# Ternary-weight gated feed-forward stage: biases accumulated on TensorE, Silu read from PSUM, one product per half, first rounding step on ScalarE

## What is computed

```python
def bit_linear(x, w, b):
    gamma_x = clip(max(abs(x), axis=-1), 1e-05)
    x_dq = clip(round(x * 127 / gamma_x), -128, 127) * gamma_x / 127
    gamma_w = clip(mean(abs(w)), 1e-05)
    w_dq = clip(round(w / gamma_w), -1, 1) * gamma_w
    return einsum('bsd,hd->bsh', x_dq, w_dq) + b
gate = silu(bit_linear(x, gate_w, gate_b))     # 256 -> 1024
val = bit_linear(x, val_w, val_b)              # 256 -> 1024
y = bit_linear(gate * val, out_w, out_b)       # 1024 -> 256, own maximum for each token
x = x + tanh(g_ffn[2]) * y
```

## Time and profile before

| What | us |
|---|---|
| median of 3 runs | 1729.23 |
| lowest, highest run | 1728.65, 1737.1 |
| the profiled execution, its own time | 1737.16 |
| span of the profiled execution | 1735.4 |
| bit stage, from the first `ints(0)` to the last `finish` | 986.9 to 1174.1 |

### The profile page before, as it was taken

One profiled execution on the slowest core, in us unless ns is written; L12 is line 12 of the kernel. 1 busy time (PEld: TensorE's weight loads), 2 busy tenths in 40 slices (PEclk: granted clock), 3 DMA queues, 4 the chain that ended last, 5 costly groups with the idle time before them and its releaser, 6 DMA issues.

```text
span 1735.4 us, 20241 instructions
## 1 busy us (share of the span) xinstructions
PE 1288.0 (74%) x6664; PEld 724.3 (42%) x6670; DVE 1071.7 (62%) x2575; ACT 455.5 (26%) x632; POOL 307.6 (18%) x287
## 2 busy tenths in 40 slices
PE   0011899999979989967767445554888889899997
PEld 0000545454434456635544322221444444455554
DVE  8988435454353356657767778884777778743222
ACT  1124212222203133322232122220443434451110
POOL 2111000000013500023344222223231222200000
PEclk9995799999989999988897666665998989899999
DMA  9000000002000010011110000002222222200001
GB/s 302 12 12 12 1 0 0 0 0 100 1 19 0 0 61 0 1 25 25 24 23 1 5 14 0 0 0 72 75 74 75 75 74 73 75 2 1 0 0 48
DMA packets 67473, 55.73 MB, mean 32 GB/s; under 512 B 23888, under 2 KB 60624, under 8 KB 67152
## 3 DMA queue, kind: packets, MB, share of 16 engines
q1 hardware_dynamic: 66768, 54.67, 10.5%
q10 hardware_dynamic: 640, 0.26, 0.1%
HBM read 39.97 MB, written 14.68 MB: 31 GB/s over the span
## 4 chain that ended last, share of the span: by engine, by line
PE 48%; DVE 19%; issue 13%; DMA 8%; POOL 6%; ACT 2%; SPq 2%; DVEq 0%; POOLq 0%; ACTq 0%
PE banks L1004 6%; PE banks L623 5%; PE banks L406 5%; PE banks L402 5%; DMA sb_work<-scratch 4%; DMA scratch<-sb_work 3%; PE banks L837 3%; PE banks L1011 3%; POOL sb_work L1429 3%; PE banks L829 3%; PE banks L413 2%; PE banks L417 2%; DVE sb_work L317 2%; PE banks L1622 1%; PE banks L1995 1%
## 5 line engine op out<-in xcount | busy, mean ns | idle before, releaser
L2233 DVE TENSOR_REDUCE sb_work<-banks 128x2 f32<-128x512 f32 x256 | 164.6, 686 | 60.6 <-PE banks L1960 56.3
L2103 ACT ACTIVATE sb_work<-banks 128x1024 f32<-128x1024 f32 x128 | 130.8, 1024 | 169.1 <-PE banks L1981 169.0
L523 DVE TENSOR_TENSOR sb_work<-sb_work,banks 128x512 f32<-128x512 f32 x72 | 49.4, 686 | 120.2 <-ACT sb_work L490 120.2
L1429 POOL TENSOR_TENSOR sb_work<-sb_work,sb_consts 128x512 f32<-128x512 f32 x64 | 66.8, 1074 | 270.0 <-ACT sb_work L1377 232.2
L1004 PE MATMUL banks<-sb_work,sb_shelf 128*128 128x512 f32 x256 | 114.4, 592 | 0.0
L623 PE MATMUL banks<-sb_work,sb_ctx_nat 128*64 128x512 f32 (+15 forms) x512 | 89.9, 510 | 7.8 <-DVE sb_work L685 7.8
L406 PE MATMUL banks<-sb_work,sb_shelf 128*128 128x512 f32 (+1 forms) x192 | 88.8, 611 | 8.6 <-DVE sb_work L566 8.6
L1960 PE MATMUL banks<-sb_work 48*128 48x256 bf16 x512 | 64.3, 295 | 41.2 <-DMA sb_work<-scratch 31.3
L1083 DVE TENSOR_TENSOR sb_work<-sb_work,banks 128x512 f32<-128x512 f32 x32 | 22.0, 688 | 110.3 <-ACT sb_work L1069 110.3
L490 ACT ACTIVATE sb_work<-banks 128x512 f32<-128x512 f32 x72 | 42.9, 596 | 178.2 <-PE banks L402 116.2
L980 POOL TENSOR_TENSOR sb_late<-sb_w2n 128x1024 f32<-128x1024 f32 x10 | 22.7, 2267 | 368.4 <-DVE sb_work L677 367.8
(11 more groups left out here) (285 smaller groups left out, 2604.9 us busy)
## 6 DMA issues: line engine op xcount, KB each, us to landing
sb_work<-scratch SPq DMA_DIRECT2D x64, 192.0 KB
scratch<-sb_work SPq DMA_DIRECT2D x32, 192.0 KB, 2.3
sb_work<-ctx_t SPq DMA_DIRECT2D x16, 256.0 KB, 4.5
scratch<-sb_work SPq DMA_DIRECT2D x32, 128.0 KB, 2.2
sb_work<-ctx_t SPq DMA_DIRECT2D x4, 512.0 KB, 3.6
sb_ctx_nat<-ctx SPq DMA_DIRECT2D x1, 2048.0 KB, 11.4
sb_raw<-wguT SPq DMA_DIRECT2D x1, 2048.0 KB, 15.7
scratch<-sb_work SPq DMA_DIRECT2D x32, 64.0 KB, 1.9
```

The lines of the kernel that those rows point to most:

```text
L1429: ins = nc.gpsimd.tensor_tensor(km_[:, hf, k, :, :], keys.unsqueeze(1).broadcast_to([P, 8, SEQ]), hm2.unsqueeze(2).broadcast_to([P, 8, SEQ ...
L2103: nc.scalar.activation(pt3[:, h % 2, :, :], o, ACT.Exp).then_inc(exp3, 1)
L2233: nc.vector.tensor_reduce(out=mx3[:, tc, k, 2 * hp:2 * hp + 2], in_=bank[u % 2].rearrange("p (h s) -> p h s", h=2), axis=AX, op=ALU.max).t ...
```

## The change

- The two bias rows are no longer broadcast. They are loaded flat, divided by the mean weight magnitude, and split in three bf16 pieces by VectorE in the convolution stage; six small DMAs on SyncE's queue (`bit_rows`) lay the pieces out as six rows of 2 x 1024.
- For each block GpSimd splits the inverse token scales in three bf16 pieces, four tiny operations (`inverse_parts`); TensorE turns them to six rows with four more transposes, and ScalarE copies these (a second copy in its `ints`).
- Each half gets two more matmuls of 512 columns, with six rows of contraction, that add bias times inverse scale to the two banks.
- ScalarE's Silu reads the gate bank in PSUM and scales on the way. VectorE makes one operation of what were two and GpSimd's product: value bank times token scale times Silu.
- `to_ints` is split: `measure` (maximum and factors) goes ahead of the next tile's product, the multiplication that rounds goes to ScalarE as `rounded`, and VectorE keeps the subtraction with output in bf16.
- GpSimd adds the output bias at the start of a block.

Its core (`...` marks what is left out):

```diff
+            if scales is not None:
+                for k in range(2):
+                    nc.vector.tensor_scalar(scales[:, k, :], qs[:, :], gam[:, k:k + 1], None, ALU.mult)
...
+        SPLITS2 = ((0, 0), (0, 1), (0, 2), (1, 0), (1, 1), (2, 0))
...
-            for dst, n, w in ((gb_b[:, 0, :], "gb2", FF2), (gb_b[:, 1, :], "vb2", FF2), (ob_b, "ob2", DIM)):
-                sp.dma_start(dst, a[n].rearrange("(o n) -> o n", o=1).broadcast_to([P, w])).then_inc(bit_b_in, 16)
+            for k, n in enumerate(("gb2", "vb2")):
+                sp.dma_start(b_flat[k * SEQ:(k + 1) * SEQ, :], a[n].rearrange("(p n) -> p n", p=SEQ)).then_inc(bit_b_in, 16)
+            sp.dma_start(ob_b, a["ob2"].rearrange("(o n) -> o n", o=1).broadcast_to([P, DIM])).then_inc(bit_b_in, 16)
+        def bit_rows(sp):
+            sp.wait_ge(b_split, 1)
+            for j, (_, piece) in enumerate(SPLITS2):
+                sp.dma_start(b_rows[j:j + 1, :, :].rearrange("p k n -> p (k n)"), b_parts[:, piece, :]).then_inc(bit_b_in, 16)
...
+            for k in range(2):
+                v = b_flat[k * SEQ:(k + 1) * SEQ, :]
+                link(nc.vector.tensor_scalar(v, v, gamr[k * SEQ:(k + 1) * SEQ, k:k + 1], None, ALU.mult))
+            for piece in range(3):
+                ins = nc.vector.tensor_copy(b_parts[:, piece, :], b_flat)
+                if piece < 2:
+                    link(ins)
+                    link(nc.vector.tensor_tensor(b_flat, b_flat, b_parts[:, piece, :], ALU.subtract))
+                else:
+                    ins.then_inc(b_split, 1)
...
                 if n >= 3:
-                    pe.wait_ge(bv_ready, 8 * b + n - 2)
+                    pe.wait_ge(bh_ready, 8 * b + n - 2)
                 elif before is not None:
-                    pe.wait_ge(bv_ready, 8 * before + (7, 8, 6)[n])
+                    pe.wait_ge(bh_ready, 8 * before + (7, 8, 6)[n])
                 for k in range(2):
                     for c in range(KC):
-                        ins = nc.tensor.matmul(bank[2 * (n % 3) + k], b_intT[:, c, t * P:(t + 1) * P],
-                                               gwT[:, k, c, f * 512:(f + 1) * 512], start=c == 0, stop=c == KC - 1)
+                        nc.tensor.matmul(bank[2 * (n % 3) + k], b_intT[:, c, t * P:(t + 1) * P],
+                                         gwT[:, k, c, f * 512:(f + 1) * 512], start=c == 0, stop=False)
+                if n == 0:
+                    pe.wait_ge(b_intT_ready, 2 * b + 2)
+                for k in range(2):
+                    ins = nc.tensor.matmul(bank[2 * (n % 3) + k], r_rows[:, t * P:(t + 1) * P],
+                                           b_rows[:, k, f * 512:(f + 1) * 512], start=False, stop=True)
                 ins.then_inc(b_gv, 1)
...
+                pe.wait_ge(r_parts_ready, b + 1)
+                pe.wait_ge(b_intT_ready, 2 * b + 1)
+                for t in range(BT):
+                    ins = nc.tensor.transpose(bf_bank(6)[0:len(SPLITS2), t * P:(t + 1) * P], r_parts[:, t, :], ident_h[:, :])
                 ins.then_inc(b_turned, 1)
...
-                    pe.wait_ge(b_intT_ready, b + 2)
...
+                act.wait_ge(b_turned, 2 * b + 1)
                 nc.scalar.activation(b_intT.rearrange("p c n -> p (c n)"), bf_bank(6), ACT.Copy).then_inc(b_intT_ready, 1)
-            def silu(b, t):
+                act.wait_ge(b_turned, 2 * b + 2)
+                nc.scalar.activation(r_rows, bf_bank(6)[0:len(SPLITS2), 0:BTOK], ACT.Copy).then_inc(b_intT_ready, 1)
+            def rounded(b, t):
+                act.wait_ge(hrec_ready, BT * b + t + 1)
+                nc.scalar.activation(bh[:, t % 2, :], bh[:, t % 2, :], ACT.Identity, bias=to_whole[:, 0:1],
+                                     scale=hrec[:, t % 2:t % 2 + 1]).then_inc(h_rounded, 1)
+            def silu(b, t, before=None):
                 for f in range(2):
-                    act.wait_ge(bg_ready, 8 * b + 2 * t + f + 1)
-                    nc.scalar.activation(bg[:, f, :], bg[:, f, :], ACT.Silu).then_inc(b_silu, 1)
+                    n = 2 * t + f
+                    if n >= 2:
+                        act.wait_ge(bh_ready, 8 * b + n - 1)
+                    elif before is not None:
+                        act.wait_ge(bh_ready, 8 * before + n + 7)
+                    act.wait_ge(b_gv, 8 * b + n + 1)
+                    nc.scalar.activation(bg[:, f, :], bank[2 * (n % 3)], ACT.Silu,
+                                         scale=tok_scale[:, 0, t:t + 1]).then_inc(b_silu, 1)
...
                 for t in range(1, BT):
+                    rounded(b, t - 1)
                     silu(b, t)
                     turned(b, t - 1)
+                rounded(b, BT - 1)
                 if not last:
                     ints(b + 1)
                 turned(b, BT - 1)
                 if not last:
-                    silu(b + 1, 0)
+                    silu(b + 1, 0, before=b)
...
+            def inverse_parts(b):
+                pool.wait_ge(b_int_ready, b + 1)
+                one = ones[:, 0:1].unsqueeze(2)
+                link(nc.gpsimd.tensor_tensor(r_parts[:, :, 0:3], qr[:, :].unsqueeze(2).broadcast_to([P, BT, 3]),
+                                             one.broadcast_to([P, BT, 3]), ALU.mult))
+                link(nc.gpsimd.tensor_tensor(r_rest, qr[:, :], r_parts[:, :, 0], ALU.subtract))
+                link(nc.gpsimd.tensor_tensor(r_parts[:, :, 3:5], r_rest.unsqueeze(2).broadcast_to([P, BT, 2]),
+                                             one.broadcast_to([P, BT, 2]), ALU.mult))
+                nc.gpsimd.tensor_tensor(r_parts[:, :, 5], r_rest, r_parts[:, :, 3], ALU.subtract).then_inc(r_parts_ready, 1)
+            inverse_parts(0)
...
+            with pool.Fori(0, BLOCKS - 1) as b:
+                link.enter(b, 3)
+                pool.wait_ge(x_done, updated(ph, b))
+                xs = x[:, bass.ds(BT * b, BT), :]
+                nc.gpsimd.tensor_tensor(xs, xs, ob_b.unsqueeze(1).broadcast_to([P, BT, DIM]),
+                                        ALU.add).then_inc(ob_added, 1)
+                inverse_parts(b + 1)
...
+            def gated(b, t):
+                if t >= 2:
+                    dve.wait_ge(bh_int_ready, BT * b + t - 1)
                 for f in range(2):
                     n = 2 * t + f
-                    if n >= 2:
-                        dve.wait_ge(bh_ready, 8 * b + n - 1)
-                    elif before is not None:
-                        dve.wait_ge(bh_ready, 8 * before + n + 7)
-                    dve.wait_ge(b_gv, 8 * b + n + 1)
-                    for k, (dst, done) in enumerate(((bg, bg_ready), (bv, bv_ready))):
-                        nc.vector.scalar_tensor_tensor(
-                            out=dst[:, f, :], in0=bank[2 * (n % 3) + k], scalar=tok_scale[:, k, t:t + 1],
-                            in1=gb_b[:, k, f * 512:(f + 1) * 512], op0=ALU.mult, op1=ALU.add).then_inc(done, 1)
-            def to_ints(b, t):
+                    dve.wait_ge(b_silu, 8 * b + n + 1)
+                    nc.vector.scalar_tensor_tensor(
+                        out=bh[:, t % 2, f * 512:(f + 1) * 512], in0=bank[2 * (n % 3) + 1],
+                        scalar=tok_scale[:, 1, t:t + 1], in1=bg[:, f, :], op0=ALU.mult, op1=ALU.mult).then_inc(bh_ready, 1)
+            def measure(b, t):
...
                 link(nc.vector.tensor_scalar(hmax[:, j], hmax[:, j], gam[:, 2:3], None, ALU.mult))
-                link(nc.vector.tensor_scalar(h, h, hrec[:, j], ROUND, ALU.mult, ALU.add))
+                dve.nop().then_inc(hrec_ready, 1)
+            def to_ints(b, t):
+                dve.wait_ge(h_rounded, BT * b + t + 1)
                 if t >= 2:
                     dve.wait_ge(bh_turned, BT * b + t - 1)
-                nc.vector.tensor_scalar(bh_int[:, t % 2, :], h, -ROUND, 127.0, ALU.add, ALU.min).then_inc(bh_int_ready, 1)
+                nc.vector.tensor_scalar(bh_int[:, t % 2, :], bh[:, t % 2, :], -ROUND, 127.0,
+                                        ALU.add, ALU.min).then_inc(bh_int_ready, 1)
...
                 for t in range(1, BT):
-                    gate_value(b, t)
+                    measure(b, t - 1)
+                    gated(b, t)
                     to_ints(b, t - 1)
                     if t > 1:
                         finish(b, t - 2)
                     if t == 1:
                         normalise(link, (b + 1) % BLOCKS)
+                measure(b, BT - 1)
                 if not last:
                     ints(b + 1)
                 to_ints(b, BT - 1)
                 finish(b, BT - 2)
                 if not last:
-                    gate_value(b + 1, 0, before=b)
+                    gated(b + 1, 0)
...
+            bit_rows(sp)
```

53 lines of the change are left out of this document (24 added, 29 removed).

## The result

The time went from 1731.65 us (median of 14 runs, 1720.2 to 1737.7) to 1747.36 us (14 runs, 1739.5 to 1753.6), a ratio of 1.0085 with an interval of 1.0065 to 1.0104: slower by some 15.7 us, above the forecast's 1732 and its range of 1721 to 1743. The profiled execution took 1745.75 us, its span is 1744.0.

What follows compares the result with a forecast made beforehand. Order within the bit stage's round was taken to decide, though VectorE looked like the bound. Rounds +3.3, opening -1.1 and last block +0.2 gave +2.4 us on 1729.2: 1732, range 1721 to 1743.

Steps and rivals of the forecast that it cites:

- S3: Round's stretch from first product matmul to tile 3's transposes: twelve matmuls instead of eight, 3.38 us before, 4.7 forecast.
- S4: Round's stretch from tile 3's transposes to the layer norm: a chain through TensorE, ScalarE and VectorE, 10.81 us before, 10.2 forecast.
- C: Rival: block's turn at the lower clock, twelve matmuls over 0.35 us each, 46.6 us a round, 1739.5 in all; chance 0.13.
- S1: Round's stretch from the end of `to_ints(b, 2)` to the next block's integers, `measure(3)` now ahead: 3.84 us before, 5.93 forecast.
- S6: Round's last stretch, to the end of `to_ints(2)`, a chain through TensorE: 10.60 us before, 8.6 forecast, 7.7 to 8.9.
- S2: Round's stretch from the next block's integers to the first product matmul, four more transposes: 2.37 us before, 2.87 forecast.
- S5: Round's stretch from layer norm to end of `to_ints(1)`, with the rounding's trip to ScalarE: 12.40 us before, 12.2 forecast.
- the tail: Bit stage's end behind the last round: TensorE's chain ends both kernels, the late `rounded` adds 0.2 us.
- The opening: Bit stage's start: up to its first norm 1.1 us longer, behind it 2.2 given back, together -1.1.
- A: Rival: longer TensorE stretches hold the higher clock through the bit stage, 39.4 us a round, 1712; chance 0.08.
- B: Rival: VectorE bounds the bit stage throughout, so all its relief shows, 37 us, 1692; chance 0.05.
- D: Rival: the Identity of `rounded` throws out Silu's function table, two loads for each of 16 tiles, +41 us, 1770; chance 0.02.

Runs made afterwards that it cites:

- rows32: The changed kernel with the added-row matmuls 32 rows deep, 26 of them zero; ratio 1.0109 against the kernel before, bit stage 187.1 us.

## Why the prediction was wrong

- *What failed* is S3, and behind it S4 in the later rounds, by the sentence "if the clock rises on the way ... I take 4.7" and the reason given against C, that the place "is now preceded by more work". The added matmuls are work of six rows, and with them the granted clock stayed down through the two halves of the turn in all three rounds, and in two of the three through the halves after it. S3 took 5.56 us for 4.7, and S4 10.59, 11.58 and 11.64 for 10.2. Over the three rounds, 7.9 us longer than forecast, S4 has 3.2, S3 2.6, S1 1.4 and S6 1.0; S2 gives 0.4 back. With 128 rows in the same places S3 is 3.8 to 4.5 and S4 9.8 to 9.9, both under the forecast, so the step that failed is the one that prices matmuls of six rows, and what they do to the clock, like those of 128. C's mechanism, the lower clock at the turn, was right and had 0.13; its 46.6 us a round was met by 46.43, 47.42 and 47.54, and its sign, a round over 46 with matmuls of 0.4 us at the block's start, came. But it priced the added matmuls like the others, without the 0.25 us a half, and its whole, 1739.5, was 8 us short.
- *The price of a six-row matmul.* 0.42 and 0.22 us were taken from rows of 48 against 128 rows. Two of them add 1.10 us to a half at the lower clock (2.78 less four at 0.42) and 0.58 at the higher (1.50 less 0.92), so 0.55 and 0.29 each: they slow their neighbours, whose weights come late. A duration is not a pitch: the earlier trace rows gave the first, and for a line whose matmuls stood among their like. The Trainium skill, in "TensorE: Matmul & The Clock Gate", section "Why this matters for your kernels", has 32 rows at the time of 128; in rows32 they came out dearer, 1.50 us a half against 1.29. The lower bound, time in proportion to rows, was rightly left out.
- *S1*, 6.41 for 5.93: a wait of 0.33 us after the measure was not priced, and the token scales took 0.27 (0.36 with the end of the last) for 0.15. *S2*, 2.72, and *S5*, 12.20, hold. *S6*, 8.95, is the dear end with the lower clock.
- *ScalarE's prices* were low (Silu 0.68 for 0.60, rounding 1.24 for 1.06, inside its bound of 1.3). The 1.06 came from an exponential over 128x1024 without scale or bias from SBUF. They explain part of *the tail*, +1.4 for +0.2: it is 9.02 with the rounding on ScalarE even with 128 rows, and 8.49 without, where the last output matmuls are as slow; with these fast it is 7.64.
- *The opening* gained the 1.1 forecast: up to the norm it is 1.4 longer (forecast 1.1), behind it 2.5 shorter (forecast 2.2). *GpSimd* took 0.50, 0.20, 0.21 and 0.21 us for its four, above the 0.11 from the earlier trace rows, and was hidden. *Outside the stage* the preparation cost nothing, as the earlier trace rows let expect.
- Of the rivals *A* fell (0.54 to 0.62 for 0.66), *B* fell (idle 73.8 us before the products), *D* fell: one load of tables in the stage, as before.
- The sum: -1.1, +10.6 in the rounds and +1.4 are the stage's 10.9 us, where the forecast had 2.4. The medians differ by 15.7 (interval 11.3 to 18.0). The other 4.8 lie outside the stage, and no run ties them to a step of the change.

## What to carry to other kernels

Before moving work to TensorE because VectorE is 82% busy, mark the round and ask which marks VectorE ends; here 38 us of its work gave 4.6. A correction by matmuls of few rows among full ones isn't cheaper for its few rows: padded with zeros to 128 it cost 4.2 us here, with six 15.5. Measure a repaired stage by its own length, and the program by its time, for the two can differ by more than the gain.

## What the runs showed of the hardware

- A half of four 128-row matmuls and two of 6, 32 or 64 rows had a mean pitch of 0.46 us at the lower clock and 0.25 at the higher, with 128 rows in all six 0.42 and 0.216.
- With six or 32 rows in the added matmuls the granted clock rose later than with 128: the halves at 1041.90 and 1044.68 ran at 1.2 GHz throughout; with 128 rows the second ran at 2.4 in that round, and the clock rose within it in the other two. At the stage's start the kernel with six rows ran five halves on end at 1.2 GHz, from 999.04 to 1012.95; with 128 rows the clock rose in the second.
- An Identity with a scale and a bias from SBUF for each partition takes 1240 ns over 128x1024, against 1057 for the exponential of the earlier trace rows, which has neither; a Silu from a bank with such a scale 677, against 597 for that of the earlier trace rows without.
